# A two-layer attention and expert kernel: its routing regrouped from six tiles to ten, and the output adds of one expert left unordered

## What is computed

```
logits = x @ wr                      # T x 8
m1, m2 = one_hot(best expert), one_hot(second best)
loc1 = cumsum(m1) - 1                # place of each token at its first expert
loc2 = cumsum(m2) - 1 + m1.sum(0)    # second choices come behind all first ones
m1, m2 = m1 * (loc1 < C), m2 * (loc2 < C)       # C = T/4 = 1024 slots an expert
t1, t2 = probabilities of the choices kept, divided by their sum
y  = 0.8 * (relu(x[slots] @ w1 + b1) @ w2 + b2) # per expert, 256 -> 1024 -> 256
out = x + t1 * y1 + t2 * y2
```

## Time and profile before

| | |
|---|---|
| time, median of 3 runs | 2146.3 us (2140.34 to 2147.84) |
| time of the profiled execution | 2144.83 us |
| its span, first to last instruction | 2143.0 us |
| TensorE's mean granted clock | 0.944 of full speed |
| TensorE busy (PE), share of the span | 1926.4 us, 90% |
| VectorE (DVE) | 1365.2 us, 64% |
| ScalarE (ACT) | 998.2 us, 47% |
| GpSimd (POOL) | 585.5 us, 27% |

### The profile page before, as it was taken

One profiled execution on the slowest core, in us unless ns is written; L12 is line 12 of the kernel. 1 busy time (PEld: TensorE's weight loads), 2 busy tenths in 40 slices (PEclk: granted clock), 3 DMA queues, 4 the chain that ended last, 5 costly groups with the idle time before them and its releaser, 6 DMA issues. The chain is left out here.

```text
span 2143.0 us, 37582 instructions
## 1 busy us (share of the span) xinstructions
PE 1926.4 (90%) x13601; PEld 1447.2 (68%) x13601; DVE 1365.2 (64%) x3573; ACT 998.2 (47%) x1958; POOL 585.5 (27%) x475
## 2 busy tenths in 40 slices
PE   4689999999999999999999999997878649999996
PEld 3456666666766666676666667665656439989986
DVE  2436667676666767676676767666775557676663
ACT  1244555555555555556555555653424223333331
POOL 1102031212303121221313122130111146677773
PEclk9679999999999999999999999997878759999998
DMA  5222443515143351514335251423120253534332
GB/s 184 84 84 77 133 150 107 168 48 168 63 158 119 116 173 64 168 63 158 105 111 167 89 167 63 149 85 115 43 89 1 79 171 81 125 87 85 48 50 23
DMA packets 205704, 225.79 MB, mean 105 GB/s; under 512 B 14168, under 2 KB 195248, under 8 KB 205520
## 3 DMA queue, kind: packets, MB, share of 16 engines
q1 hardware_dynamic: 191136, 206.40, 29.3%
q0 software_dynamic: 14384, 16.99, 5.0%
HBM read 150.82 MB, written 72.52 MB: 104 GB/s over the span
## 5 line engine op out<-in xcount | busy, mean ns | idle before, releaser
L1218 DVE TENSOR_REDUCE MX<-bank 128x2 f32<-128x512 f32 x768 | 493.6, 684 | 171.4 <-PE bank L851 169.8
L1467 ACT ACTIVATE PT<-bank 128x512 f32<-128x512 f32 x768 | 416.7, 597 | 253.2 <-PE bank L888 250.7
L851 PE MATMUL bank<-KS,QS 32*128 32x256 f32 (+1 forms) x1536 | 198.0, 337 | 44.2 <-DVE MX L1218 43.6
L888 PE MATMUL bank<-QM,KS 32*128 32x256 f32 (+1 forms) x1536 | 197.4, 336 | 37.8 <-ACT PT L1467 27.3
L903 PE MATMUL bank<-PT,VA 128*32 128x256 f32 x3072 | 214.2, 398 | 8.5 <-ACT PT L1467 7.5
L851 PEld LDWEIGHTS bank<-KS,QS 32*128 32x128 f32 (+1 forms) x1536 | 120.4, 193 | 132.7 <-DVE MX L1218 70.9
L888 PEld LDWEIGHTS bank<-QM,KS 32*128 32x128 f32 (+1 forms) x1536 | 121.1, 193 | 125.3 <-issue 66.8
L1819 ACT ACTIVATE hid<-bank,b1T 128x512 f32<-128x512 f32 x128 | 87.8, 686 | 231.1 <-PE bank L1771 231.1
L703 POOL TENSOR_TENSOR rrB<-uwB,cst 128x4 f32<-128x4 f32 x16 | 16.3, 1018 | 595.5 <-DVE uwB L1187 595.5
L1784 PE MATMUL bank<-W2h,hTh 128*128 128x256 f32 x512 | 144.0, 281 | 0.0
L1784 PE MATMUL bank<-W2l,hTh 128*128 128x256 f32 x512 | 142.7, 279 | 0.0
(11 more groups left out here) (323 smaller groups left out, 3778.4 us busy)
## 6 DMA issues: line engine op xcount, KB each, us to landing
W<-in_L_ffn_w_dram SPq DMA_DIRECT2D x48, 1024.0 KB, 7.4
KS<-k_dram SPq DMA_DIRECT2D x64, 512.0 KB, 5.8
QS<-q_dram SPq DMA_DIRECT2D x64, 512.0 KB, 6.0
k_dram<-qTQ SPq DMA_DIRECT2D x32, 256.0 KB, 2.5
q_dram<-pTQ SPq DMA_DIRECT2D x32, 256.0 KB, 7.3
k_dram<-PRP SPq DMA_DIRECT2D x32, 256.0 KB, 2.5
q_dram<-cTP SPq DMA_DIRECT2D x32, 256.0 KB, 2.6
X<-in_x_dram SPq DMA_DIRECT2D x16, 256.0 KB, 6.5
```

Source lines behind the costliest of these rows:

```text
L851: x = mm(halves(u)[:, r, :], Q[strip, slot, r * P:(r + 1) * P], K[strip, slot, :], start=True, stop=True)
L888: x = mm(halves(2 + u)[:, kc, :], K[strip, slot, kc * P:(kc + 1) * P], QM[strip, slot // 2 % 2, slot % 2, :], start=True, stop=True)
L1218: v.tensor_reduce(MX[:, slot % 4, j, :], halves(u), AX, ALU.max, negate=True).then_inc(h.maxed, 1)
L1467: s_.activation(PT[:, n % 8, :, :], halves(2 + n % 2), ACT.Exp, scale=h.scale).then_inc(h.exp, 1)
```

## The change

- Groups of ten, ten, eight and two tiles in place of six, six, six, six, four and two (`ROUTED`); tiles 30 and 31 stay where they are. A run is one group: D2 waits for the first group of ten in round 15 and the second waits for D2. The strings EARLY, LATE and LAST are new.
- Running sums by TensorE: the totals of tile k are multiplied by ones into the columns of all later tiles, and the triangular product is summed on top, n+2 products a group. VectorE then adds one row `runs` to all counts, and one row to `runs`.
- The slot-row tiles H are written by GpSimd (`route_pool`), with two semaphores more: `low` (VectorE has `Mi` and `hi`) and `spot` (GpSimd has H). The last group writes them on VectorE as before (`inside=False`).
- A group has 16 steps of two or three operations in place of seven; the table product lies in the first half of bank 5, and `route_chances` is a step of its own.
- Ten tiles need five buffers of each kind, so free weight buffers are lent to them, and the start of the routing waits for B1's last product in place of an earlier one.
- In `experts` each parity of units has its own semaphore for its adds. GpSimd waits only at an expert's first add, and there for all adds of earlier experts; adds of one expert, which go to different rows, wait for nothing. Rows of empty slots lie out of bounds and are dropped. VectorE waits for the adds of the unit before last in its buffer; `s_adding` is gone.

```diff
-ROUTED = {-1: (((0, 6), (6, 6)), ((12, 6), (18, 6))), 0: (((24, 4),), ((28, 2),)), 1: ((), ())}
-N_ROUTE = 7
-N_R = 1 + N_ROUTE * 4
...
+ROUTED = {-1: (((0, 10),), ((10, 10),)), 0: (((20, 8),), ((28, 2),)), 1: ((), ())}
+N_ROUTE = 16
+N_R = 1 + N_ROUTE * 2
...
+EARLY = "QPQPPSPSQSTPSRRSPETERRRRERSVPSQQQERTSEVRSEQTPRSRPRRVSEPRQSPESPPRSTRESVESPESPQEVSPVSPTPQSEQPPESRSPQSPEQTSPEQEVQRERPQVRPRRERRQQTRRRRERPVEPEVVRREPERRVQ"
...
-    GROUP = 6
+    GROUP = 10
...
-        self.runs = sb("r_runs", [P, n + 1, 2 * NE])
...
+        self.runs = sb("r_runs", [P, 2 * NE])
...
-def route_tensor(t, R, g, t0, n, cst, ones, bank, A, H):
+def route_tensor(t, R, g, t0, n, cst, ones, bank, A, H, inside=True):
 
     w = 2 * R.NE
     yield
-    M = R.M[:, t0:t0 + n, :, :].rearrange("p n c e -> p (n c e)")
+    M = R.M[:, t0:t0 + n, :, :].rearrange("p n c e -> p n (c e)")
+    yield from idle(4)
     t.wait_ge(R.chosen, g + 1)
     if g:
         t.wait_ge(R.added, g)
-    t.matmul(bank[:, 0:n * w], cst[:, C_TRI:C_TRI + P], M, start=True, stop=True)
-    t.matmul(bank[:, P:P + n * w], ones, M, start=True, stop=True).then_inc(R.ranked, 1)
+    counts = bank[:, 0:(n + 1) * w].rearrange("p (n x) -> p n x", x=w)
+    t.matmul(counts[:, 0, :], cst[:, C_TRI:C_TRI + P], M[:, 0, :], start=True, stop=True)
+    for k in range(n):
+        x = t.matmul(counts[:, k + 1:n + 1, :], ones, M[:, k, :].unsqueeze(1).broadcast_to([P, n - k, w]), start=k == 0, stop=k == n - 1)
+        if k == 0:
+            t.matmul(counts[:, 1:n, :], cst[:, C_TRI:C_TRI + P], M[:, 1:n, :], start=False, stop=False)
+    x.then_inc(R.ranked, 1)
     yield
-    yield from idle(3)
+    yield from idle(8)
     t.wait_ge(R.hot, g + 1)
+    if inside:
+        t.wait_ge(R.spot, g + 1)
     for c in range(2):
         for k in range(n):
-            x = t.matmul(bank[:, (2 + c) * P:(3 + c) * P], A[(2 * k + c) // 4][:, (2 * k + c) % 4, :], H[(2 * k + c) // 4][:, (2 * k + c) % 4, :], start=k == 0, stop=k == n - 1)
+            x = t.matmul(bank[:, c * P:(1 + c) * P], A[(2 * k + c) // 4][:, (2 * k + c) % 4, :], H[(2 * k + c) // 4][:, (2 * k + c) % 4, :], start=k == 0, stop=k == n - 1)
     x.then_inc(R.tabled, 1)
     yield
     yield
...
+    yield from idle(14)
+
+
+def route_pool(g_, R, g, n, H):
+
+    w, NE = 2 * R.NE, R.NE
+    hi, rows = R.hi[:, 0:2 * n, :], R.Mi[:, 0:n, :, :, :].rearrange("p n c i e -> p (n c) (i e)")
+    yield from idle(12)
+    for k in range(0, 2 * n, 4):
+        m = min(4, 2 * n - k)
+        if k == 0:
+            g_.wait_ge(R.low, g + 1)
+        x = g_.tensor_tensor(H[k // 4][:, 0:m, :].rearrange("p k (m h) -> p k m h", h=NE), rows[:, k:k + m, :].unsqueeze(3).broadcast_to([P, m, w, NE]),
+                             hi[:, k:k + m, :].unsqueeze(2).broadcast_to([P, m, w, NE]), ALU.mult)
+        if k + 4 >= 2 * n:
+            x.then_inc(R.spot, 1)
+        if k in (4, 8):
+            yield
+    if 2 * n <= 8:
+        yield from idle(1 if 2 * n > 4 else 2)
+    yield
+    yield
...
+        yield
         link(v.tensor_reduce(R.kx[:, 0:n], cut(R.key), AX, ALU.max))
         link(tt(dst, cut(R.key), each(R.kx), ALU.is_equal))
 
...
+    yield
+    yield from first_max(L, M[:, :, 0, :])
+    yield
     link(v.scalar_tensor_tensor(cut(R.l2), M[:, :, 0, :], -3.0e38, L, ALU.mult, ALU.add))
     link(v.tensor_reduce(R.mx[:, 0:n], cut(R.l2), AX, ALU.max))
-    first_max(cut(R.l2), M[:, :, 1, :])
+    yield
+    yield from first_max(cut(R.l2), M[:, :, 1, :])
...
     w = 2 * NE
     v.wait_ge(R.ranked, g + 1)
-    for k in range(n):
-        link(tt(R.runs[:, k + 1, :], R.runs[:, k, :], bank[:, P + k * w:P + (k + 1) * w], ALU.add))
     loc = R.loc[:, 0:n, :, :]
     flat = lambda x: x.rearrange("p n c e -> p n (c e)")
-    link(tt(flat(loc), bank[:, 0:n * w].rearrange("p (n x) -> p n x", x=w), cut(R.runs), ALU.add))
-    link(v.tensor_copy(R.runs[:, 0, :], R.runs[:, n, :]))
+    link(tt(flat(loc), bank[:, 0:n * w].rearrange("p (n x) -> p n x", x=w), R.runs[:, :].unsqueeze(1).broadcast_to([P, n, w]), ALU.add))
+    link(tt(R.runs[:, :], R.runs[:, :], bank[:, n * w:(n + 1) * w], ALU.add))
+    yield
     link(tt(loc, loc, M, ALU.mult))
     link(v.tensor_reduce(rank, loc, AX, ALU.add))
...
-    link(tt(hi, ge[:, :, 0:NE], ge[:, :, 1:NE + 1], ALU.subtract))
+    yield
+    if inside and g:
+        v.wait_ge(R.spot, g)
     link(v.tensor_reduce(lo, ge[:, :, 0:NE], AX, ALU.add))
     link(v.scalar_tensor_tensor(lo, lo, -float(P), q, ALU.mult, ALU.add))
+    link(tt(hi, ge[:, :, 0:NE], ge[:, :, 1:NE + 1], ALU.subtract))
+    yield
     Mi = R.Mi[:, 0:n, :, :, :]
     for i in range(2):
         link(tt(Mi[:, :, :, i, :], M, R.ids[:, t0:t0 + n, i].unsqueeze(2).unsqueeze(3).broadcast_to([P, n, 2, NE]), ALU.mult))
+    if inside:
+        v.sem_inc(R.low, 1)
     yield
     rows = Mi.rearrange("p n c i e -> p (n c) (i e)")
     for k in range(0, 2 * n, 4):
         m = min(4, 2 * n - k)
-        link(tt(H[k // 4][:, 0:m, :].rearrange("p k (m h) -> p k m h", h=NE), rows[:, k:k + m, :].unsqueeze(3).broadcast_to([P, m, w, NE]),
-                hi[:, k:k + m, :].unsqueeze(2).broadcast_to([P, m, w, NE]), ALU.mult))
+        if not inside:
+            link(tt(H[k // 4][:, 0:m, :].rearrange("p k (m h) -> p k m h", h=NE), rows[:, k:k + m, :].unsqueeze(3).broadcast_to([P, m, w, NE]),
+                    hi[:, k:k + m, :].unsqueeze(2).broadcast_to([P, m, w, NE]), ALU.mult))
         link(tt(A[k // 4][:, 0:m, :], lo[:, k:k + m].unsqueeze(2).broadcast_to([P, m, P]), R.iota[:, :].unsqueeze(1).broadcast_to([P, m, P]), ALU.is_equal))
+        if k == 8:
+            yield
+    if 2 * n <= 8:
+        yield
     v.sem_inc(R.hot, 1)
 
-    yield
     yield
     v.wait_ge(R.tabled, g + 1)
     table = R.table[:, :, :, :, :].rearrange("p c i e h -> p (c i e h)")
-    link(tt(table, table, bank[:, 2 * P:4 * P], ALU.add))
+    link(tt(table, table, bank[:, 0:2 * P], ALU.add))
     v.sem_inc(R.added, 1)
-    if chances:
+    yield
+    if inside:
         route_chances(v, R, g, t0, n)
     yield
...
+            def routing(r):
+                if r == B - 1:
+                    yield
+                for run in routed(r):
+                    for k, t0, n in run:
+                        yield from route_pool(g, routes, k, n, spots)
...
-                    wait(v, pe, "B1", B - 1, "nT")
+                    wait(v, pe, "B1", B - 1, "v")
...
-        R.work_in(cut_from(sb("route_work", [P, 1024])[:, :]))
+        R.work_in(cut_from(sb("route_work", [P, 2048])[:, :]))
...
-            sp.wait_ge(s_add, 16 + 16 * UNITS * HT4)
+            sp.wait_ge(s_pad, 16)
+            for i in range(2):
+                sp.wait_ge(s_add[i], UNITS // 2 * 16 * HT4)
...
-            g.sem_inc(s_adding, 1)
...
-                    g.wait_ge(s_add, n * 16 + 16)
-                    if r == 0:
-                        g.sem_inc(s_adding, 1)
+                    if r == 0 and u % NH == 0 and u:
+                        for i in range(2):
+                            g.wait_ge(s_add[i], u // 2 * 16 * HT4)
                     g.indirect_dma_start(out=out, out_offset=bass.IndirectOffsetOnAxis(ap=put[:, n:n + 1], axis=0),
                                          in_=yo[u % 2][:, r, :], in_offset=None,
-                                         bounds_check=T + P - 1, oob_is_err=True, compute_op=ALU.add).then_inc(s_add, 16)
+                                         bounds_check=T - 1, oob_is_err=False, compute_op=ALU.add).then_inc(s_add[u % 2], 16)
...
-                v.wait_ge(s_adding, u + 1)
+                if u >= 2:
+                    v.wait_ge(s_add[b], u // 2 * 16 * HT4)
```

More of the change, by code:

```diff
@@ L215, in route_start_vector @@
     v.memset(R.table[:, :, :, :, :].rearrange("p c i e h -> p (c i e h)"), 0.0)
-    v.memset(R.runs[:, 0, :], -1.0)
+    v.memset(R.runs[:, :], -1.0)
     link(v.memset(R.step[:, NE:NE + 1], float(R.CAP)))
@@ L253, in route_scalar @@
     yield
-    yield from idle(5)
+    yield from idle(14)
[17 more added lines that the diff above has]
+    yield
 def route_chances(v, R, g, t0, n):
@@ L268, in route_chances, with route_vector @@
     link(tt(R.p[:, t0:t0 + n, :], cut(R.pe), R.zs[:, 0:n].unsqueeze(2).broadcast_to([P, n, 2]), ALU.mult))
-def route_vector(v, R, g, t0, n, cst, logits, bank, A, H, chances=True):
+def route_vector(v, R, g, t0, n, cst, logits, bank, A, H, inside=True):
     NE, CAP = R.NE, R.CAP
@@ L408, in layers @@
         raw = {n: PT[:, i, :, :] for i, n in enumerate(("WqA", "WkA", "WvA", "WoA", "WqC", "WkC"))}
-        routes.work_in(cut_from(*(x[:, :, :].rearrange("p t d -> p (t d)") for x in (X0, XBA))))
-        hot, spots = ([x[:, :, :].rearrange("p t (k x) -> p (t k) x", x=P) for x in xs] for xs in ((CXA, NQ, cxTQ), (PRQ, pTQ, cTQ)))
+        routes.work_in(cut_from(*(x[:, :, :].rearrange("p t d -> p (t d)") for x in (X0, XBA, MA))))
```

(15 more changed lines are left out.)

10 lines of the change are left out of this document (4 added, 6 removed).

## The result

The changed kernel takes 2135.07 us (median of 19 runs, 2122.88 to 2140.74) where the kernel before takes 2147.03 (19 runs): a ratio of 0.9939, 95% interval 0.9926 to 0.9951. That is 12 us less. The forecast was 38 us less, and the range did not hold the time. A second set of runs of the changed kernel gave 0.9929 (0.9904 to 0.9955). The profiled execution took 2136.49 us, with a span of 2134.7.

The account below looks back on a forecast made before the run. Round 15 was taken as bound by a chain of routing groups and D2 through PSUM bank 5. 2144.8 - 32 + 2 + 0.5 - 7.9 = 2107.4, forecast 2108 us, range 2094 to 2131.

Parts of the forecast that it names:

- round 15 (15a + 15b): Round 15, routing in two groups of ten for four of six: 32 us less, bounds 8 and 45.
- round 16 (16a + 16b): Round 16, groups of 8 and 2 for 4 and 2: +2 us, bounds -5 and +9.
- round 17: Round 17, no routing and an order differing by one swap of heads: 0, bounds +-2 us.
- end of the adds: End of the expert stage: adds of one expert no longer wait for each other, -7.9 us, bounds -5 and -8.
- so 20 us go, which is what group 4 costs today: Round 15's second half, 51 us today: keeping one routing group leaves 31 us.
- The second way, by occupancy: Round 15: VectorE's remaining 84.7 us of work over 0.76 occupancy gives 111 us, a gain of 36.
- Counting on TensorE: Routing groups of ten: counting records grow from 4 to 24, 2.6 to 6.1 us; 4 us in the serial sum.
- Slot rows: Routing groups of ten: GpSimd writes slot rows at 1.27 us each, 6.4 us a group; contention costs the chain nothing.
- rival 1: Routing in rounds 15 and 16: hand-off to GpSimd becomes the new wait, 2122 us; chance 0.20.
- Rival 3: Routing in rounds 15 and 16: GpSimd's slot rows make it slower, 2160 us at 5 us each; chance 0.05.
- The 2118 us: Forecast if one-hot tiles and slot rows exclude each other and alternate, by the skill's rule: about 2118 us.
- Rival 2: Round 15: routing only fills holes between heads, so only the end is gained, 2137 us; chance 0.20 not applicable, stated 0.13.

Follow-up runs that it names:

- tens_old: Kernel before with unordered adds and groups of ten, ten, eight and two, but old written orders and steps, sums and slot rows on VectorE: ratio 0.9979.
- old_orders: Changed kernel with all three order strings made from those of the kernel before: 2165.77 us, ratio 1.0071.
- stores_later: Changed kernel with running sums on VectorE, round 16's end reordered, and GpSimd's D2 row operations and following stores moved to their thread's end: 2128.86 us, ratio 0.9891.
- light: Changed kernel with round 15's first group cut from ten tiles to two and round 16's first from eight to four, twelve tiles left unrouted: ratio 0.9881.
- rows_vector: Changed kernel with the slot rows back on VectorE, written orders kept: ratio 0.9951.
- hold_clock: Changed kernel with 14 more products of 128x256 on TensorE in round 17's first half, results unused: ratio 0.9939.

## Why the prediction was wrong

| term | predicted | measured | from |
|---|---|---|---|
| round 15 (15a + 15b) | -32 | -19 | 145.1, 147.0 before; 125.6, 125.8, 129.4 with the changed routing |
| round 16 (16a + 16b) | +2 | +8 | 84.9, 81.8; 93.7, 90.6, 90.0 |
| round 17 | 0 | +4.6 | 42.5, 41.7; 46.7 three times |
| last group | +0.5 | +1.2 | 26.7, 26.6; 27.9, 28.0, 27.5 |
| end of the adds | -7.9 | -8.1 | 16.7; 8.6 |
| sum | -37.4 | -13 | |

The end was right to 0.2 us, step by step: adds that follow their tiles by less than a microsecond, and the same 7.8 us behind the last.

**Round 15.** The step that failed is "so 20 us go, which is what group 4 costs today", with the reading that groups and D2 through bank 5 fill the round without a hole. They do, but they are not what ends it. Taking a group out of this half under the old order gave 2 us (`tens_old`, 50.6 to 48.8), since TensorE's stream still had heads and layer products queued behind the routing steps. A wait that ended last was read as the bound; the sum did not ask what else was still to be done when it goes. The new order supplies that, and is the part of the change that I priced at nothing: 51.4 us becomes 36.3 by the strings alone (`old_orders` against the changed kernel), and the whole round 151.8 becomes 125.6. Then the estimate of 31 us for this half is missed by 5. Of its terms the choosing is furthest off, 7.1 us where 3 was counted, but with 5.5 the half was no shorter (`stores_later`), so what makes the 5 us is open. The first half was priced at 11 us by VectorE's share (12 us over 0.76 is 15.8, not 15) and gave 4 (95.1 to 91.1, means of two traces and of three, which is within the scatter); by `light` the two tiles fewer are worth 1.7 of it, and the new order put more of the layers' work into this half. The second way, by occupancy, failed in the same step: VectorE's work fell to 87 us, close to the 85 forecast, but the round did not shrink with it, and VectorE's share of it fell from 0.76 to 0.69.

**Counting on TensorE.** Priced at 4 us a group, it took 4.8 us in the first group (1483.19 to 1487.98) and 5.5 in the second, and taking it off again gains 1.2 to 2.4 us in 15b. The prediction had its length near enough and left out that it is one unbroken step in front of the heads.

**Slot rows.** 1.07 us where 1.27 was taken. The step with the rows was longer all the same: from the first row to the last tile 10.2 us in the first group (1501.21 to 1511.39) and 9.6 in the second (1573.36 to 1582.94), where 6.4 was counted and stalls were taken as free. In the first group tiles and rows stretched each other; in the second VectorE's first tile came 4.6 us after the first row, behind layer work. But GpSimd's last row ended 3.7, 4.4 and 2.7 us ahead of VectorE's last tile in the groups of ten, ten and eight, so TensorE never waited for GpSimd, and rival 1's mechanism did not come; nor are the rows cheaper on VectorE (`rows_vector`). Rival 3 is out. The Trainium skill's rule (SBUF — State Buffer, Who interferes with whom) held for the tiles, compares with two SBUF inputs beside GpSimd's reads, in that both were stretched. It held in part only, as one of each came every 1.47 us, less than the 1.76 us of both alone. The 2118 us that the prediction made of it are as far off in the other terms as the forecast.

**Round 16.** "Shorter steps let the chain's other VectorE work through earlier" failed: at the end of the round the new order lets routing through earlier, ahead of the norm that the layer chain waits for. With the norm ahead again, and with GpSimd's operations beside it and their stores moved, 16b is 19.5 us (`stores_later`), below the 20.5 to 21.1 of before. 16a is 65.4 to 68.8 us where 61.3 and 63.8 stood before. The four tiles more can be most of that (`tens_old`) or a third (`light` against `after_again`); it is open.

**Round 17.** Priced at nothing, as its work is the same. It ran at 1.2 GHz throughout in the changed routing, in four traces of four (with `light`), and with round 16's end, the counting or the rows changed it did not. That the loss goes with the clock is shown, by the same records at either level and by `hold_clock`. What in round 16 decides it was not found.

Rival 2's 2137 us is near the time, but not for its reason: round 15 did shorten, by 19 us, and rounds 16 and 17 gave 13 of it back.
